# Inverse norms of queries and keys: one power on GpSimd in place of Ln, Exp and a Newton step

## The reference, cut to what matters

```python
def l2norm(t):
    return t / jnp.maximum(jnp.linalg.norm(t, axis=-1, keepdims=True), 1e-12)

qkv = x @ Wqkv                        # 128 -> 3 * 1024
q, k, v = split(qkv, 3); each to (b, 16 heads, n, 64)
q = l2norm(q) * qs
k = l2norm(k) * ksc
q = q * cos * scale + rotate_half(q) * sin * scale
k = k * cos / scale + rotate_half(k) * sin / scale
out = softmax(mask(q @ k.T * 8.0)) @ v      # in windows of 32
```

## Time and profile before

| | |
|---|---|
| median of 3 runs | 3594.57 us (3592.3 to 3594.88) |
| span of the profiled execution | 3598.4 us, 3.8 us above that median |
| PE busy | 3482.8 us, 97% |
| DVE busy | 3160.0 us, 88% |
| ACT busy | 3061.0 us, 85% |
| POOL busy | 2352.0 us, 65% |
| chain that ended last | PE 62%, ACT 19%, issue 10%, DVE 5% |
| period of one step (middle of the run) | 33.4 us |
| granted PE clock | full (0.9 to 1.0 in all slices) |

### The profile page before, as it was taken

One profiled execution on the slowest core, in us unless ns is written; L12 is line 12 of the kernel. 1 busy time (PEld: TensorE's weight loads), 2 busy tenths in 40 slices (PEclk: granted clock), 3 DMA queues, 4 the chain that ended last, 5 costly groups with the idle time before them and its releaser, 6 DMA issues.

```text
span 3598.4 us, 95666 instructions
## 1 busy us (share of the span) xinstructions
PE 3482.8 (97%) x33868; PEld 2390.4 (66%) x33868; DVE 3160.0 (88%) x5848; ACT 3061.0 (85%) x5121; POOL 2352.0 (65%) x1607
## 2 busy tenths in 40 slices
PE   8999899999999999999999999999999999999998
PEld 6777466666666666666666666666666666666666
DVE  6998889888988988888888898888889888888986
ACT  5766688888888888888888888888888888888886
POOL 2001677777777777777777677777777777777774
PEclk9999999999999999999999999999999999999999
DMA  2000011112211112211112111112111112211112
GB/s 63 0 0 0 21 34 39 38 33 54 52 34 34 39 36 52 50 40 33 34 40 53 46 39 38 32 36 58 47 33 39 38 33 55 52 33 34 39 37 54
DMA packets 182965, 136.67 MB, mean 38 GB/s; under 512 B 97612, under 2 KB 135632, under 8 KB 182800
## 3 DMA queue, kind: packets, MB, share of 16 engines
q1 hardware_dynamic: 180019, 125.00, 14.8%
q10 hardware_dynamic: 2781, 9.51, 0.9%
HBM read 19.04 MB, written 2.10 MB: 6 GB/s over the span
## 4 chain that ended last, share of the span: by engine, by line
PE 62%; ACT 19%; issue 10%; DVE 5%; SPq 1%; POOL 1%; DMA 1%; ACTq 0%; DVEq 0%; POOLq 0%
PE ps L1302 12%; PE ps L1389 10%; PE ps L1356 10%; PE ps L1344 7%; PE ps L1379 4%; PE ps L1370 4%; PE ps L1160 3%; ACT L750 3%; ACT area L603 2%; DVE area L987 2%; ACT G L609 2%; ACT L609 2%; ACT area L618 2%; ACT area L625 2%; PE ps L1295 2%
## 5 line engine op out<-in xcount | busy, mean ns | idle before, releaser
L1302 PE MATMUL ps<-Wqkv,xsT 128*128 128x512 f32 x2304 | 1112.5, 605 | 8.7 <-ACT area L638 3.8
L449 POOL TENSOR_TENSOR area<-area,tab 128x512 f32<-128x512 f32 x768 | 970.0, 1273 | 146.7 <-ACT area L618 146.1
L1302 PEld LDWEIGHTS ps<-Wqkv,xsT 128*128 128x128 f32 x2304 | 391.2, 189 | 351.4 <-issue 295.0
L462 POOL TENSOR_TENSOR area<-area,lsum 128x1024 f32<-128x1024 f32 x192 | 365.5, 1904 | 383.2 <-DVE lsum L916 383.2
L456 POOL TENSOR_TENSOR AQb<-AQb,area 128x1024 f32<-128x1024 f32 x192 | 455.2, 2371 | 15.1
L456 POOL TENSOR_TENSOR area<-area 128x1024 f32<-128x1024 f32 x192 | 455.0, 2370 | 9.0 <-DVE area L976 1.5
L618 ACT ACTIVATE area<-ps 128x1024 f32<-128x1024 f32 x384 | 393.6, 1025 | 66.2 <-PE ps L1302 55.1
L1389 PEld LDWEIGHTS ps<-kbd,area 128*32 128x32 f32 x12288 | 313.2, 109 | 196.1 <-issue 113.4
L1344 PE MATMUL ps<-BD,area 128*64 128x128 f32 x6144 | 421.5, 279 | 17.7 <-issue 11.3
L1344 PEld LDWEIGHTS ps<-BD,area 128*64 128x64 f32 x6144 | 329.4, 137 | 158.8 <-issue 100.2
L1389 PE MATMUL ps<-kbd,area 128*32 128x128 f32 x12288 | 415.6, 276 | 17.0 <-ACT kbd L648 5.7
(11 more groups left out here) (136 smaller groups left out, 6630.6 us busy)
## 6 DMA issues: line engine op xcount, KB each, us to landing
BD<-area SPq DMA_DIRECT2D x1344, 64.0 KB, 2.0
Vx<-area SPq DMA_DIRECT2D x384, 32.0 KB, 1.9
Wqkv<-ffn_Wqkv ACTq DMA_DIRECT2D x18, 512.0 KB, 4.0
BB<-area SPq DMA_DIRECT2D x384, 16.0 KB, 1.8
x2s<-x2s SPq DMA_DIRECT2D x96, 56.0 KB, 2.0
Wo<-ffn_Wo SPq DMA_DIRECT2D x6, 512.0 KB, 4.3
W<-ffn_W SPq DMA_DIRECT2D x6, 341.0 KB
x2s<-x2s SPq DMA_DIRECT2D x96, 0.2 KB, 1.7
```

The lines of the kernel that those rows point to most:

```text
L449: pool.tensor_tensor(b4[:, :, here], q4[:, :, there], s4[:, :, here], ALU.mult).then_inc((s_bq, s_bk)[j], 1)
L462: pool.tensor_tensor(p3, p3, lsum[:, 1, :].unsqueeze(2).broadcast_to([P, HEADS, 2 * WIN]), ALU.mult).then_inc(s_pn, 1)
L1302: last = mm(PJ[:, b * 512:(b + 1) * 512], xsT[:, par, t * P:(t + 1) * P], Wqkv[:, w0:w0 + 512], start=True, stop=True)
```

## The change

The Ln and the Exp on ACT go, as do the second flooring and the Newton step on DVE. POOL raises the floored sums to the power -0.5, with a constant tile of -0.5 as second operand, 128 x 32 elements for queries and keys of a tile together. DVE copies the result from SBUF to the place in PSUM from which `over_norms` reads it. In POOL's queue the power of tile 0 stands ahead of `normalise(n-1, 1)`, that of tile 1 behind `rotated(n-1, 1, 0)`.

```diff
+        minus_half = sb("minus_half", [P, 2 * HEADS])
...
+            pool.memset(minus_half[:, :], -0.5).then_inc(i_guess, 1)
+            pool.wait_ge(i_guess, 3)
...
+            def norm_roots(n, t):
+
+                T = 2 * n + t
+                need(pool, s_fl, T + 1)
+                pool.tensor_tensor(ss[:, 3 + t, :], ss[:, 1, :], minus_half[:, :], ALU.pow).then_inc(s_iv, 1)
...
                     sines(n - 1, 1, 0, True)
                     rotated(n - 1, 1, 0)
+                    norm_roots(n - 1, 1)
                     sines(n - 1, 1, 1, True)
                     rotated(n - 1, 1, 1)
...
                     sines(n, 0, 1, True)
+                    norm_roots(n, 0)
                 if mid:
                     normalise(n - 1, 1)
...
-            def norm_guess(n, t):
-                T = 2 * n + t
-                need(act, s_fl, T + 1)
-                act.activation(ss[:, 2, :], ss[:, 1, :], ACT.Ln).then_inc(s_lg, 1)
-                need(act, s_lg, T + 1)
-                act.activation(ss[:, 3 + t, :], ss[:, 2, :], ACT.Exp, bias=guess_c, scale=-0.5).then_inc(s_iv, 1)
...
                     k_evac(n - 1, 0, 1)
-                    norm_guess(n - 1, 1)
...
                     act.preload_act_table_set(TABLE_SET)
-                if head:
-                    norm_guess(n, 0)
...
-                dve.tensor_scalar(small[:, t, 0, :], ss[:, 0, :], NORM_FLOOR * NORM_FLOOR, None, ALU.max).then_inc(s_nw, 1)
...
             def inverse_norms(n, t):
 
                 T = 2 * n + t
-                v, w, y, z = small[:, t, 0, :], small[:, t, 1, :], small[:, t, 2, :], ss[:, 3 + t, :]
-                need(dve, s_nw, 4 * T + 1)
                 need(dve, s_iv, T + 1)
-                dve.tensor_tensor(w, v, z, ALU.mult).then_inc(s_nw, 1)
-                dve.wait_ge(s_nw, 4 * T + 2)
-                dve.tensor_tensor(w, w, z, ALU.mult).then_inc(s_nw, 1)
-                dve.wait_ge(s_nw, 4 * T + 3)
-                dve.scalar_tensor_tensor(y, w, NEWTON, z, ALU.subtract, ALU.mult, reverse0=True).then_inc(s_nw, 1)
+                dve.tensor_copy(small[:, t, 2, :], ss[:, 3 + t, :]).then_inc(s_nw, 1)
...
-                need(dve, s_nw, 4 * T + 4)
+                need(dve, s_nw, T + 1)
```

More of the change, by code:

```diff
@@ L377, in _ @@
             pool.wait_ge(i_pad, 2)
-            pool.wait_ge(i_guess, 2)
+            pool.memset(minus_half[:, :], -0.5).then_inc(i_guess, 1)
+            pool.wait_ge(i_guess, 3)
             for g in range(4):
```

## The result

The changed kernel takes 4456.3 us (median of 4 runs, 4424.6 to 4475.6) against 3594.7 us before. The ratio is 1.2388 (95% interval 1.2336 to 1.2440): 862 us slower. The prediction said 3665 and a range of 3550 to 3870. The sign was right, the size wrong by a factor of twelve.

The account below looks back on a forecast made before the run. PE, 97% busy, was taken as the bound. A 1.83 us power less 1.1 cover loses 0.73 us a step, PE's 0.3 gain not realised; 96 steps make +70 us, so 3665 us against the median, range 3550 to 3870.

Parts of the forecast that it names:

- d = 1.8: Duration in us of one new POOL power of 32 columns, worked out as 1.83 from an estimated 24 elementary steps.
- The upper bound: On POOL, a power costing 24 whole instructions, 6.1 us: 8.85 us a step, +850, about 4445 us.
- all above d = 3.1: Rival of a long POOL power, both tiles' cycles counting in full: +254 us (3849) at 3 us duration; chance 0.17.
- The two rules of the Trainium skill: Two estimates of the POOL power's duration, about 0.4 us and 2.8 us, speaking for opposite signs of the result.
- The form of the sum: Each tile's power costs a step its duration less its cover; beyond 2.25 us both tiles count and the slope is two.
- cover: Waiting time already in the queues behind a POOL power that absorbs its duration before the step gets longer.
- Tile 1's cover: DVE's waits for PE, 0.99 us a step, plus about 0.15 until ACT would notice: 1.1 us.
- Tile 0's: Cover at tile 0: 1.1 us before POOL's normalising, plus 1.15 at its wait for raw keys, together 2.25 us.
- the other path: Tile 0's power delays DVE's transposing by its duration less 1.1 us, and `gated(2)`, where PE has some tenths of cover.
- Tile 1's path: Late keys' `over_norms`, row maxima, exponential, normalising, transposing, BD, PE's value sums; loses the duration less 1.1 us a step.
- rival (a): Quick POOL power, below 0.9 us: PE gains 0.3 us a step at tile 0's keys, -29 us, about 3566; chance 0.34.
- What would show it: Expected trace signs: DVE's keys wait for POOL, its PE waits vanish, PE's BD wait grows 0.7 us, period about 34.1 us.

Follow-up runs that it names:

- experiment 6: Changed kernel plus unread PE matmuls ahead of the feed-forward output and of the turn of tile 1's keys: 4318.0 us.
- experiments 1: Changed kernel with the power replaced by a multiplication of the same size at both tiles (wrong numbers): 3581.7 us, ratio 0.9961.
- 5: Kernel before, without a power, with tile 0's Ln and Exp moved on ACT ahead of the first two GELUs and the table load: 3581.6 us.
- 11: Kernel before, tile 0's Ln and Exp moved ahead of the GELUs and its Newton step ahead of DVE's transposing of tile 1's softmax: 3581.9 us.
- 12: Changed kernel with a power of 8 of 32 columns at tile 1 only and the multiplication at tile 0 (wrong numbers): 3622.4 us.

## Why the prediction was wrong, point by point

- **The duration of the power is the step that failed.** "I take d = 1.8", from 24 elementary steps at 2.14 ns a column. It is 5.44 us. A column costs as much as 75 such steps. The upper bound, 24 whole instructions or 6.1 us, did hold it, and its price (about 4445) lay near the result, but I gave all above d = 3.1 only 0.17. Between two ends a factor of 24 apart I chose by a count of 24 steps that no row supported and no run has shown since; the runs show only 160 ns a column. The two rules of the Trainium skill that I weighed ("GPSIMD Engine Reference", section 3.1: three operations a cycle, d about 0.4; section 7: 4 cycles for each dependent operation, d about 2.8) were worked out with the same count; the measured 5.44 us agrees with neither.
- **The form of the sum** was right: no loss within a cover, then one step-time lost for each microsecond beyond. With the measured d it gives (5.44 - 1.1) + (5.44 - 2.25) = 7.53 us a step, 723 us, 4318 us; experiment 6, with the clock kept up, measured 4318.0. To the last digit that is luck. Tile 1's cover was 1.24 (said 1.1; counted from the kernel before, as I did, it is 1.4). Tile 0's was 1.49, not 2.25: I had put its loss at POOL's wait for the raw keys and called the other path, over transposing, `gated(2)` and the feed-forward output, a loss beside the larger one. The runs showed that this path binds first and nearly in series with tile 1's. The 46 us that the places share, and the 15 us that the change gains elsewhere, made up for it.
- **Tile 1's path was right up to DVE's subtraction (L906) and wrong behind it.** I had it go on over the exponential, normalising, transposing and BD to PE's value sums. PE's wait for BD did not grow (55.5 us in 70, before 56.7 in 72, 0.79 each time in both). The loss went over the mask write and the query copies on ACT, two instructions that my account leaves out, to PE's turn of tile 1's keys: 241.3 us in 89. That the cover came out near 1.1 all the same is due to the part that was right, DVE's waits for PE ahead of that point.
- **Missing: PE's clock.** 138 us. I looked at the granted clock of before, found it full, and did not ask what it would be once PE waits 3 us twice a step. It makes even the upper bound's agreement partly an accident.
- **The removal** (rival (a)) was rightly seen as PE's wait for tile 0's keys and nothing else, but taken at 29 us where it is 15; the waits of the matmul itself were the measure, not those of the weight load. That work spared on ACT and DVE buys nothing was right (experiments 1, 5 and 11).
- **What would show it:** the wait of L987 (now L980) for POOL appears, and so does L462 (now L470) coming late with PE waiting at the feed-forward output. I had listed the latter as a sign that the loss lies at tile 0's power; it lies at both. DVE's wait for PE at L901 was to be gone; it is in experiments 6 and 12, but in the changed kernel, with the low clock, it is 100.1 us in 70. Two signs did not appear: the exponential (now L613) waited for L906 only 0.9 us in 2 cases, since the mask write ahead of it does that waiting, and PE's wait for BD stayed.

The account of the 862 us by medians: -15 for all that is not the power's duration, +379 tile 0, +403 tile 1, -46 shared, +138 clock, sum 859; the remaining 3 us is the difference between the medians of before. The 46 is no measurement of its own but what is left when the two single prices are set against both together. Where they overlap is not settled; no run isolates it.

## What to carry to other kernels

An operation without a row in the trace is to be bounded in both directions, and if the ends differ in sign and by a factor of 24, the forecast is a wide one and no middle is better founded than another; one run of the bare instruction at four sizes would have settled it. Before work is moved off an engine, look for what it waits behind: here a swap of two calls on ACT, ahead of a table load, gave all of the gain that the move could give. And a new wait on PE is priced twice, by its length and by the slower matmuls behind it; the second price has to be measured with all the waits in place, since 158 and 132 us alone were 138 together.

## What the runs showed of the hardware

- GpSimd's power takes 160 ns a column of 128 partitions in float32 and 0.36 us fixed (8 to 128 columns), 5.43 us for 32 with exponent -0.5 and the same with 2 (one call each, on a constant), and 5.43 to 5.46 us over the 192 calls on this kernel's sums. A multiplication of 32 columns takes 0.25 us.
- After PE had waited 2.7 us in the changed kernel, its granted clock was 0.50 in the next 3.5 us and four matmuls of 512 columns took 3.62 us in place of 1.88. Unread bf16 matmuls in the wait brought the mean clock of the profiled execution from 0.908 to 0.996 and the median time down by 138 us, though a wait of 1.66 us remained behind them.
